# Softmax attention: the product of probabilities and values issued in two halves of 256 query columns

## The chip, the cores and the metric

The kernel runs on one core of one Trainium2 chip. The metric is the device time of one execution in microseconds (us), median of several runs. The profile is of one execution.

## The reference

Two blocks, each an attention-like mixer gated by a mixture of experts. The change touches only the softmax attention of the first block, on 8 sequences of 512 tokens, 128 features, 16 heads of 8:

```python
xn = _layernorm(x, axis=-1)
qkv = xn @ w_qkv + b_qkv                                   # 8 x 512 x 384
attn = jnp.einsum('bhqd,bhkd->bhqk', q, k) * hd ** (-0.5)  # hd = 8, 16 heads
attn = jax.nn.softmax(attn, axis=-1)
out = jnp.einsum('bhqk,bhkd->bhqd', attn, v)
s = out @ w_proj + b_proj
x = x + s * silu(experts(xn))
```

The second block is a linear attention with running sums and another set of experts.

## The kernel before, in words

The attention stage runs over 32 quarters u; a quarter is one sequence b and one group g of four heads. A loop `steps` calls `attend(u, g, b, now)` on each engine for u from -3 to 32; each engine has its own program, and semaphores order them. A quarter has four steps t (128 keys each), and a step has four pairs of scores, one for each head j; i = 4t + j counts pairs in a quarter.

In a pair TensorE issues two matmuls, on two different strips of 32 rows of its array: L1022 gives the scores of quarter u with keys on the partitions, 128 keys x 512 queries, in one of three banks (2, 3, 4); L1028 gives scores of quarter u + 2 with queries on the partitions, in one of three other banks (0, 1, 7). ScalarE turns the first into probabilities (L1297, `exp_set`). VectorE reduces the second to the negative row maxima (L1667, `max_set`), which go into the scores two quarters later as extra rows. The pair i may start when the exponential and the reduction of the pair three before it are done (`read_before`), since there are three banks of each.

The probabilities of a step are four tiles of 128 keys x 512 queries, in one of two buffers (t % 2). `output(u, g, t, even)` (L1119 to L1124) multiplies them with the values: four matmuls, one for each head, on four strips of 32 columns of the array, into the one bank 5, where they are added up over the four steps. The data are fp32, so that each matmul shows as two records. It is issued in step t + 1, behind the third pair (j == 2), and for t = 3 in the first step of the next quarter. It waits for the last exponential of its step, and the first of a quarter waits also until ScalarE has copied the accumulator of the quarter before (L1309, `o_read`). `pv_mm` counts the products; ScalarE waits for it before it overwrites a buffer of probabilities, and before the copy.

Behind the fourth pair of a step TensorE does other work of the stage: in t = 0 the transpose of the maxima (L1052); in t = 1 the transposes of the accumulator (L1066), which VectorE normalizes (L1691, L1693); in t = 2 and 3, depending on g, the projections of a later sequence (L324 to L326 through `project`), the projection of the values and its transposes (L1106), or transposes and the matmuls of the output projection (L1081, L1099). In the first and last quarters, filler matmuls (`keep_busy`, L1112) stand there too. VectorE also computes the low part of the maxima (m_lo, L1682) in t = 1, the low parts of projections (L1656) and the biased result (L1698). The order in each engine is fixed by hand as the code stands. GpSimd spreads tokens over experts' slots and splits the experts' weights meanwhile; SyncE's queue brings in the keys and queries of coming quarters.

Of the kernel before, what the change touches and what calls it, by code (L numbers as in the profile page):

```python
# [33 lines left out]
SEQ = 512  # L34
# [4 lines left out]
GROUPS = 4  # L39
# [7 lines left out]
def build(nc, x, w_qkv, b_qkv, w_proj, b_proj, router_w, w1, v1, w2, ffn_bias,  # L47
# [21 lines left out]
    with ctx:  # L69
# [3 lines left out]
        def sem(name):  # L73
            return ctx.enter_context(nc.semaphore(name))

        ps = ctx.enter_context(nc.psum_tensor("ps", [P, 8, 512], F32))
# [98 lines left out]
        def stage():  # L175
# [22 lines left out]
        probs = take(2, 4, SEQ)  # L198
# [9 lines left out]
        vaug = take(2, QT, HEADS, 32)  # L208
# [86 lines left out]
        st_mm, exp_set, pv_mm, o_read, oT_mm, onorm_set = (  # L295
            sem("st_mm"), sem("exp_set"), sem("pv_mm"), sem("o_read"), sem("oT_mm"), sem("onorm_set"))
# [88 lines left out]
        def bank_of(i):  # L385


            return 1 if i == 15 else i % 3

        def head_rows(tile, g, j):  # L390

            return tile[32 * j:32 * j + 32, g, :]

        def max_head(j):

            return (j + 2) % 4

        def read_before(i):

            return {0: -3, 1: 0, 2: -1, 15: 14}.get(i, i - 2)  # L400
# [510 lines left out]
        def _(pe):  # L911
# [90 lines left out]
            def attend(u, g, b, now):  # L1002
                v, g2 = u + 2, (g + 2) % GROUPS
                for t in range(4):
# [9 lines left out]
                    for j in range(4):  # L1014
                        i = t * 4 + j
                        if now.main:

                            if now.first and i == 0:
                                pe.wait_ge(e_set[0], 2)
                            if not (now.first and i < 3):  # L1020
                                pe.wait_ge(exp_set, u * 16 + read_before(i))
                            pe.matmul(ps[:, 2 + bank_of(i), :], head_rows(Ks, g, j)[:, t * P:(t + 1) * P],  # L1022
                                      head_rows(Qs, g, j), start=True, stop=True).then_inc(st_mm, 1)
                        if now.max:
                            if not (isinstance(v, int) and v * 16 + i < 3):
                                pe.wait_ge(max_set, v * 16 + read_before(i))
                            j2 = max_head(j)
                            pe.matmul(ps[:, (0, 1, 7)[bank_of(i)], :], head_rows(Qs, g2, j2)[:, t * P:(t + 1) * P],  # L1028
                                      head_rows(Ks, g2, j2), start=True, stop=True).then_inc(s_mm, 1)
                        if j == 2 and t == 0 and now.tail:  # L1030
                            output(u - 1, (g + 3) % GROUPS, 3, now.tail_even)
                        if j == 2 and t >= 1 and now.main:
                            if t == 1:

                                if not now.first:
                                    pe.wait_ge(o_read, u)
                                pe.wait_ge(vaug_set, b + 1)
                            output(u, g, t - 1, now.even)
                    if t == 0 and now.low:


# [15 lines left out]
                    if t == 1 and now.tail:  # L1057
# [7 lines left out]
                        for q in range(QT):  # L1065
                            mm = pe.transpose(ps[:, 6, q * P:(q + 1) * P], o_sb[:, q * P:(q + 1) * P], ident[:, :])  # L1066
# [5 lines left out]
                    if t == 2:  # L1072
# [5 lines left out]
                        if g == 0 and now.tail:  # L1078
                            pe.wait_ge(onorm_set, u)
                            for q in range(QT):  # L1080
                                mm = pe.transpose(ps[:, 6, q * P:(q + 1) * P], onorm[:, q, :], ident[:, :])  # L1081
# [10 lines left out]
                    if t == 3:  # L1092
# [3 lines left out]
                        if g == 0 and now.tail:  # L1096
                            pe.wait_ge(onT_set, b)
                            for q in range(QT):
                                mm = pe.matmul(ps[:, 6, q * P:(q + 1) * P], onT[:, q * P:(q + 1) * P], wproj[:, :],  # L1099
                                               start=True, stop=True)  # L1100
                            mm.then_inc(out_mm, 1)
                        if g == 3 and now.load:

                            pe.wait_ge(vT_set, b + 2)
                            for q in range(QT):
                                mm = pe.transpose(ps[:, 6, q * P:(q + 1) * P], vT[:, q * P:(q + 1) * P], ident[:, :])  # L1106
# [9 lines left out]
                split3(pe, ps[:, bank, :], wq_hi[:, which, :], wq_lo[:, which, :],  # L1116
                       seq_of(xT_hi, b), seq_of(xT_lo, b)).then_inc(proj_mm, 1)

            def output(u, g, t, even):  # L1119

                pe.wait_ge(exp_set, u * 16 + (4 * t + 4))
                for j in range(4):
                    mm = pe.matmul(ps[32 * j:32 * j + 32, 5, :], vaug[:, even, t, 4 * g + j, :],  # L1123
                                   probs[:, t % 2, j, :], start=(t == 0), stop=(t == 3))  # L1124
                mm.then_inc(pv_mm, 1)

# [127 lines left out]
            pe.wait_ge(pool_con, 19)  # L1256
            norm(0)
            steps(pe, attend)
            experts(0)
            pe.wait_ge(y_read[0], TILES)  # L1260
# [694 lines left out]
```

## Time and profile before

| | |
|---|---|
| median of 3 runs | 1088.25 us (1087.11 to 1091.65) |
| span of the profiled execution, first to last instruction | 1101.2 us |
| attention with products | from 86.9 to 473.9 us of it |
| busy shares, whole span | TensorE 89%, VectorE 77%, ScalarE 56%, GpSimd 52% |

The profile of the one execution gives its span, and no other time for it; the runs of the median were without a profile. Times of rows are us from the start of the span. Busy time of TensorE is the union of matmuls, whose ends are modelled. A granted clock of 1.00 is 2.4 GHz, one of 0.50 is 1.2 GHz.

### The profile page before, as it was taken

To read this page: it belongs to the slowest core of one execution; us is meant where nothing else is said; L and a number is where in the kernel's file an instruction comes from. 1 tells how busy PE (TensorE), PEld (TensorE's weight loads), DVE (VectorE), ACT (ScalarE), POOL (GpSimd) and SP (SyncE) were. 2 spreads that over 40 slices of the span, in tenths; PEclk is the share of its full clock that TensorE was granted. 3 is DMA by queue.
4 is the path that set the end of the run, shared out by engine and by line. 5 is a ranking of instruction groups with operands and counts; after the bars stand their busy time and mean duration, and the time that the engine had idled before them with its cause. 6 is when DMAs were issued, how large, how long until landed. Compare 5 with 4: busy or idle time off the path is not lost. (4 is left out here: it accounts for less than half of the span.)

```text
span 1101.2 us, 18065 instructions
## 1 busy us (share of the span) xinstructions
PE 980.5 (89%) x5608; PEld 634.8 (58%) x5608; DVE 852.7 (77%) x1910; ACT 620.6 (56%) x1248; POOL 572.2 (52%) x631
## 2 busy tenths in 40 slices
PE   5789999999999999989999964999996999999960
PEld 4542344343434344368888853756655888888850
DVE  7556899999979999435555548699992899999975
ACT  6115788888868888843333326333333666777642
POOL 7220687443435442015555556378782576777770
PEclk9995999999979999999999985699997999999985
DMA  6736566353535532216666635034312677687719
GB/s 209 300 104 193 160 193 209 101 169 113 170 101 170 178 116 88 87 58 195 207 197 187 205 95 146 20 108 126 93 44 82 180 214 208 208 224 220 218 56 236
DMA packets 121521, 170.37 MB, mean 155 GB/s; under 512 B 18801, under 2 KB 80594, under 8 KB 118354
## 3 DMA queue, kind: packets, MB, share of 16 engines
q1 hardware_dynamic: 94290, 110.94, 35.1%
q0 software_dynamic: 18688, 54.08, 14.3%
q10 hardware_dynamic: 8448, 4.20, 1.5%
q8 instruction: 45, 0.74, 0.3%
q14 instruction: 50, 0.41, 0.1%
HBM read 106.71 MB, written 63.76 MB: 155 GB/s over the span
## 5 line engine op out<-in xcount | busy, mean ns | idle before, releaser
L1667 DVE TENSOR_REDUCE nmax<-ps 128x1 f32<-128x512 f32 x512 | 324.8, 683 | 50.2 <-PE ps L1028 45.6
L1297 ACT ACTIVATE stage<-ps 128x512 f32<-128x512 f32 x512 | 274.4, 594 | 75.6 <-PE ps L1022 69.6
L841 POOL DMA_INDIRECT token_y<-stage,ids_now x184 | 182.7, 993 | 130.0 <-DVE stage L1723 58.3
L1028 PE MATMUL ps<-stage,stage 32*128 32x512 f32 x512 | 189.1, 521 | 14.1 <-DVE nmax L1667 12.8
L1022 PE MATMUL ps<-stage,stage 32*128 32x512 f32 x512 | 172.3, 496 | 9.0 <-ACT stage L1297 7.5
L797 POOL DMA_INDIRECT slots_x<-xn,pos x128 | 154.5, 1207 | 40.7 <-issue 39.6
L1168 PEld LDWEIGHTS ps<-stage,stage 128*128 128x128 f32 (+1 forms) x1288 | 164.9, 191 | 13.5 <-issue 1.8
L1168 PE MATMUL ps<-stage,stage 128*128 128x128 f32 (+1 forms) x1288 | 170.9, 275 | 1.5 <-issue 1.2
L1022 PEld LDWEIGHTS ps<-stage,stage 32*128 32x128 f32 x512 | 70.3, 188 | 158.0 <-ACT stage L1297 125.9
L324 PE MATMUL ps<-stage,stage 128*128 128x512 f32 x322 | 141.1, 438 | 3.6 <-issue 3.6
L1123 PE MATMUL ps<-stage,stage 128*32 128x512 f32 x1024 | 144.2, 637 | 0.0
L326 PE MATMUL ps<-stage,stage 128*128 128x512 f32 x322 | 127.8, 397 | 0.0
L325 PE MATMUL ps<-stage,stage 128*128 128x512 f32 x322 | 127.1, 395 | 0.0
L1350 ACT ACTIVATE stage<-ps 128x512 f32<-128x512 f32 (+1 forms) x69 | 41.2, 597 | 104.8 <-PE ps L326 83.0
L1028 PEld LDWEIGHTS ps<-stage,stage 32*128 32x128 f32 x512 | 75.6, 194 | 37.7 <-DVE nmax L1667 30.2
L1787 DVE TENSOR_TENSOR stage<-ps,stage 128x512 f32<-128x512 f32 (+1 forms) x69 | 47.5, 689 | 61.6 <-PE ps L326 36.9
L1352 ACT ACTIVATE stage<-ps,ebcol 128x512 f32<-128x512 f32 x92 | 63.2, 687 | 52.8 <-PE ps L326 24.1
L1791 DVE SCALAR_TENSOR_TENSOR stage<-stage,stage 128x512 f32<-128x512 f32 x92 | 71.3, 774 | 23.3 <-ACT stage L1355 16.9
L326 PEld LDWEIGHTS ps<-stage,stage 128*128 128x128 f32 x322 | 59.8, 186 | 15.6
L324 PEld LDWEIGHTS ps<-stage,stage 128*128 128x128 f32 x322 | 60.4, 188 | 11.9 <-issue 2.3
L325 PEld LDWEIGHTS ps<-stage,stage 128*128 128x128 f32 x322 | 60.4, 187 | 8.2
L1355 ACT ACTIVATE stage<-ps,ebcol 128x512 f32<-128x512 f32 x92 | 63.2, 687 | 0.6 <-PE ps L326 0.6
(226 smaller groups left out, 1537.4 us busy)
## 6 DMA issues: line engine op xcount, KB each, us to landing
stage<-halves_w SPq DMA_DIRECT2D x23, 1024.0 KB
stage<-halves_w SPq DMA_DIRECT2D x23, 704.0 KB
stage<-slots_x SPq DMA_DIRECT2D x46, 260.0 KB
stage<-q_halves SPq DMA_DIRECT2D x32, 256.0 KB
halves_w<-stage POOLq DMA_DIRECT2D x16, 512.0 KB
k_halves<-stage SPq DMA_DIRECT2D x24, 256.0 KB
q_halves<-stage SPq DMA_DIRECT2D x24, 256.0 KB
stage<-k_halves SPq DMA_DIRECT2D x128, 48.0 KB
```

The costliest lines, as they stand in the source:

```text
L324: pe.matmul(out_ap, w_hi_ap, x_hi_ap, start=start, stop=False)
L325: pe.matmul(out_ap, w_hi_ap, x_lo_ap, start=False, stop=False)
L326: return pe.matmul(out_ap, w_lo_ap, x_hi_ap, start=False, stop=stop)
L797: pool.indirect_dma_start(out=slots_x[L], out_offset=bass.IndirectOffsetOnAxis(ap=pos[:, c:c + 1], axis=0), in_=xn[:, t, :], in_offset=Non ...
L841: pool.indirect_dma_start(out=token_y, out_offset=bass.IndirectOffsetOnAxis(ap=ids_now[:, r, q:q + 1], axis=0), in_=ysb[:, r, q, :], in_of ...
L1022: pe.matmul(ps[:, 2 + bank_of(i), :], head_rows(Ks, g, j)[:, t * P:(t + 1) * P], head_rows(Qs, g, j), start=True, stop=True).then_inc(st_m ...
L1028: pe.matmul(ps[:, (0, 1, 7)[bank_of(i)], :], head_rows(Qs, g2, j2)[:, t * P:(t + 1) * P], head_rows(Ks, g2, j2), start=True, stop=True).th ...
L1123: mm = pe.matmul(ps[32 * j:32 * j + 32, 5, :], vaug[:, even, t, 4 * g + j, :], probs[:, t % 2, j, :], start=(t == 0), stop=(t == 3))
L1168: mm = pe.matmul(ps[:, 5 + r, q * P:(q + 1) * P], hT[0:M, par, q * P:(q + 1) * P], wdn[0:M, r, f, :], start=(f == 0 and q == 0), stop=(f = ...
L1297: act.activation(probs[:, t % 2, j, :], ps[:, 2 + bank_of(i), :], ACT.Exp, scale=SCALE).then_inc(exp_set, 1)
L1667: dve.tensor_reduce(nmax[:, g % 2, at:at + 1], ps[:, (0, 1, 7)[bank_of(i)], :], AX, ALU.max, negate=True).then_inc(max_set, 1)
L1791: dve.scalar_tensor_tensor(hT[:, par, :], gsig[:, par, :], 1.0, gact[:, par, :], ALU.add, ALU.mult).then_inc(h_set[L], 1)
```

## The change

Each product is issued in two halves: query columns 0 to 255 behind the second pair (j == 1), columns 256 to 511 behind the fourth (j == 3), in the same step as before. A half has four matmuls of 256 columns. The wait for the exponentials stands before the first half, `pv_mm` is increased after the second. Only the first half of the first step starts the accumulation; only the second half of the last ends it. The work that stood behind the fourth pair now stands behind the second half.

```diff
-                        if j == 2 and t == 0 and now.tail:
-                            output(u - 1, (g + 3) % GROUPS, 3, now.tail_even)
-                        if j == 2 and t >= 1 and now.main:
-                            if t == 1:
+                        if j in (1, 3) and t == 0 and now.tail:
+                            output(u - 1, (g + 3) % GROUPS, 3, now.tail_even, j // 2)
+                        if j in (1, 3) and t >= 1 and now.main:
+                            if t == 1 and j == 1:
 
                                 if not now.first:
                                     pe.wait_ge(o_read, u)
                                 pe.wait_ge(vaug_set, b + 1)
-                            output(u, g, t - 1, now.even)
+                            output(u, g, t - 1, now.even, j // 2)
...
-            def output(u, g, t, even):
-
-                pe.wait_ge(exp_set, u * 16 + (4 * t + 4))
+            def output(u, g, t, even, part):
+
+                if part == 0:
+                    pe.wait_ge(exp_set, u * 16 + (4 * t + 4))
+                c = slice(part * SEQ // 2, (part + 1) * SEQ // 2)
                 for j in range(4):
-                    mm = pe.matmul(ps[32 * j:32 * j + 32, 5, :], vaug[:, even, t, 4 * g + j, :],
-                                   probs[:, t % 2, j, :], start=(t == 0), stop=(t == 3))
-                mm.then_inc(pv_mm, 1)
+                    mm = pe.matmul(ps[32 * j:32 * j + 32, 5, c], vaug[:, even, t, 4 * g + j, :],
+                                   probs[:, t % 2, j, c], start=(t == 0 and part == 0), stop=(t == 3 and part == 1),
+                                   skip_group_check=True)
+                if part == 1:
+                    mm.then_inc(pv_mm, 1)
```

## Rows read from the trace of the kernel before

**Rows 1.** The page: the span, and the granted clock in 40 slices (tenths).

```profile
span 1101.2 us, 18065 instructions
...
PEclk9995999999979999999999985699997999999985
```

**Rows 2.** Windows of the attention stage: stretch, length, busy us, granted clock.

```profile
88.00:108.00 20.00, 18.80 (x81) 5.90 (x77) 11.69 (x21) 9.59 (x19) 2.07 (x4) 0.50 0.60 185
116.00:304.00 188.00, 183.36 (x1192) 76.01 (x1190) 174.63 (x313) 154.68 (x305) 109.27 (x136) 1.00 0.52 159
...
320.00:442.00 122.00, 118.48 (x780) 49.41 (x776) 113.81 (x204) 101.04 (x199) 46.79 (x53) 1.00 0.43 132
```

Behind the length stand TensorE, its weight loads, VectorE, ScalarE and GpSimd, then the clock, DMA share and GB/s.

**Rows 3.** Groups of lines, 148 to 292 us: busy, mean ns, idle before.

```profile
L1667 DVE TENSOR_REDUCE nmax<-ps 128x1 f32<-128x512 f32 x195 | 123.5, 683 | 8.3 <-PE ps L1028 5.9 <-issue 1.5
L1297 ACT ACTIVATE stage<-ps 128x512 f32<-128x512 f32 x195 | 104.6, 593 | 20.0 <-PE ps L1022 17.2 <-issue 0.6
```

**Rows 4.** Timeline of TensorE, a plain step: start, length, line, idle before.

```profile
254.47 0.50 PE L1028 MATMUL ps<-stage,stage 32*128 32x512 f32 x1
254.90 1.07 PE L1123 MATMUL ps<-stage,stage 128*32 128x512 f32 x8
255.90 0.49 PE L1022 MATMUL ps<-stage,stage 32*128 32x512 f32 x1
...
257.64 1.07 PE L1123 MATMUL ps<-stage,stage 128*32 128x512 f32 x8
...
259.07 0.28 PE L1052 MATMUL ps<-ident,nmax 128*16 128x128 f32 x1
259.28 0.50 PE L1022 MATMUL ps<-stage,stage 32*128 32x512 f32 x1
```

**Rows 5.** Timeline of VectorE over the same steps.

```profile
251.46 0.25 DVE L1691 RECIPROCAL rden<-ps 128x16 f32<-128x16 f32 x1
...
251.94 4.27 DVE L1667 TENSOR_REDUCE nmax<-ps 128x1 f32<-128x512 f32 x7
256.46 2.57 DVE L1667 TENSOR_REDUCE nmax<-ps 128x1 f32<-128x512 f32 x4 [0.25 <-PE ps L1028]
```

**Rows 6.** Timeline of TensorE: transposes of the maxima, one a quarter (four of them).

```profile
116.19 0.28 PE L1052 MATMUL ps<-ident,nmax 128*16 128x128 f32 x1
...
295.25 0.28 PE L1052 MATMUL ps<-ident,nmax 128*16 128x128 f32 x1
...
324.53 0.28 PE L1052 MATMUL ps<-ident,nmax 128*16 128x128 f32 x1
...
441.83 0.27 PE L1052 MATMUL ps<-ident,nmax 128*16 128x128 f32 x1
```

**Rows 7.** Timeline of TensorE, a step at the half clock.

```profile
91.06 1.94 PE L1123 MATMUL ps<-stage,stage 128*32 128x512 f32 x8
92.92 0.79 PE L1022 MATMUL ps<-stage,stage 32*128 32x512 f32 x1
...
94.53 0.79 PE L1028 MATMUL ps<-stage,stage 32*128 32x512 f32 x1
95.25 1.94 PE L1123 MATMUL ps<-stage,stage 128*32 128x512 f32 x8
```

**Rows 8.** Timeline of TensorE: a projection behind the fourth pair.

```profile
169.37 0.51 PE L324 MATMUL ps<-xT_hi,wq_hi 128*128 128x512 f32 x1
...
170.27 0.50 PE L1022 MATMUL ps<-stage,stage 32*128 32x512 f32 x1
...
170.61 0.39 PE L1022 MATMUL ps<-stage,stage 32*128 32x512 f32 x1
```

**Rows 9.** Timeline of TensorE's weight loads: those of one product.

```profile
252.02 0.16 PEld L1123 LDWEIGHTS ps<-stage,stage 128*32 128x32 f32 x8 [0.24 <-issue]
```

**Rows 10.** Timeline of TensorE: filler matmuls in the last quarters.

```profile
458.45 0.73 PE L1112 MATMUL ps<-xT_hi,wq_hi 128*128 128x512 f32 x2
459.12 0.69 PE L1022 MATMUL ps<-stage,stage 32*128 32x512 f32 x3
```

## The prediction

> **What bounds the kernel now.** I read the page first [rows 1]: one span of 1101.2 us, and TensorE's granted clock at 9 or more of 10 in nearly all slices, with a slice of 5 at the start of the attention stage (slice 4, 82 to 110 us) and one of 7 in its middle (slice 12). Then the windows of the attention stage [rows 2]. At the full clock, 116 to 304 us and 320 to 442 us, TensorE shows 97% busy, VectorE 93%, ScalarE 82%. Three engines so close together say that none is alone the bound: the work goes in a loop through them. The groups of lines [rows 3] say where VectorE stops: its reduction (L1667) takes 683 ns, and what ends most of the idle time before it is a score matmul of TensorE (L1028). ScalarE's exponential (593 ns) waits for TensorE longer still. So I read the timeline of TensorE through one plain step, a step being the four pairs of scores of one t [rows 4].
>
> The loop is this. The last pair before the product (L1123) starts at 254.47; the product starts 0.43 us later, at 254.90, when that pair is done. The next pair starts 1.00 us after it, at 255.90, and takes 0.49. VectorE has run seven reductions in one train without a gap (251.94, 4.27 us) and then has nothing for 0.25 us: its next one begins at 256.46 [rows 5], 0.07 after the pair's end. Its reduction takes 0.68, and the third pair after may only start then, because there are three banks for each kind of score. 0.43 + 1.00 + 0.49 + 0.07 + 0.68 = 2.67 us, and the products stand 2.74 apart (254.90, 257.64); what is left, 0.07, is the release's (I use 0.05 below). The seven reductions give a pitch of (4.27 - 0.68) / 6 = 0.60 us, so four take 2.40. A plain step is thus 0.3 us longer than VectorE needs, and the whole product standing between two pairs is the reason: three banks cover 1.8 us, and from the release of the pair before the product to the data of the pair behind it 0.43 + 1.00 + 0.49 + 0.12 = 2.04 us pass.
>
> **What a half costs.** No row shows a product of 256 columns. But the whole one stands at both levels of the clock: 1.00 us from its start to the next pair at 2.4 GHz [rows 4] and 92.92 - 91.06 = 1.86 us at 1.2 GHz [rows 7]. The part that goes with the clock is the difference, 0.86 us at the full clock, and 0.14 stays. A half is then 0.43 + 0.14 = 0.57 us, at the half clock 0.86 + 0.14 = 1.00. Bounds: 0.50 (everything halves) and 1.00 (nothing does). I take 0.57, since 86% of the whole was seen to follow the clock, as streamed columns do.
>
> The change adds 128 blocks (32 quarters, four products each). Each further block needs the pair before it drained: 0.43 from that pair's start [rows 4], where pairs otherwise follow at once or at 0.2 to 0.3. What this comes to if it is not hidden is a part of rival (a).
>
> **The plain step after the change.** First half behind the second pair: that pair starts when the reduction three before is done (call it 0, plus 0.05); half from 0.48 to 1.05; third pair's data at 1.54, wanted by VectorE at 1.80. Fourth pair: released at 1.20, so it starts at 1.25; second half 1.68 to 2.25; next pair's data at 2.74, wanted at 3.00. Both come 0.26 us early, so VectorE sets the pace: 2.40 to 2.45 for 2.74, a gain of 0.30. The first half has to wait for the fourth exponential of the step before, which the third pair waited for anyhow; with ScalarE's pitch (under 0.6) it ends near 0.3, before 0.48. Behind this wait stand the third pair's matmuls of both kinds and all that follows; they are hidden by the same 0.26.
>
> Written as a chain from the fourth pair: 0.43 + 0.57 + X + 0.49 + 0.07 + 0.60 + 0.05 = 2.21 + X, where X is what TensorE does behind the step's last pair. The maxima's transpose gives X = 0.21 (259.07 to 259.28 [rows 4]): 2.42, still a gain of 0.30. The projection gives 170.27 - 169.37 = 0.90 [rows 8], so 3.11. Before, TensorE's own path there is 0.43 + 1.00 + 0.43 + 0.90 + 0.33 = 3.09 (0.33 is the step from the first two pairs to a third, 170.27 to 170.61 [rows 8]). These steps win nothing; the same holds for the others with X of 0.6 to 1.1 (transposes, out projection).
>
> Steps of four quarters: 16. Four have t = 1, where VectorE adds m_lo, the reciprocal and the normalization (251.46 to 251.94 is 0.48 us for the latter two [rows 5]) and is the bound already: nothing. Six at t = 2 or 3 have a large X (two projections, the value projection and its transposes, two steps of the output path): nothing. Six are plain or have X = 0.21: 6 x 0.30 = 1.8 us per four quarters. At the full clock with the reductions running lie 15 quarters from 116.19 to 295.25 and 10 from 324.53 to 441.83 [rows 6]: 25 / 4 x 1.8 = 11.3 us.
>
> **At the half clock** [rows 7] products stand 4.19 apart (91.06, 95.25). After: a pair's drain is 0.72 (94.53 to 95.25), so 2 x 0.72 + 2 x 1.00 = 3.44, with some 0.15 for a trailing pair 3.6: a gain of 0.6 a step. The stretch at the start holds at least 20 us at 0.50 [rows 2], 20 / 4.19 = 4.8, five steps. In the middle, the two quarters from 295.25 to 324.53 [rows 6] are 5.4 us longer than two at the mean of the fifteen before ((295.25 - 116.19) / 15 = 11.94); at 4.19 - 2.74 = 1.45 a step that is 3.7, of which I count three: 3.0 + 1.8 us.
>
> **The rest at nothing.** In the last two quarters there are no reductions, and TensorE puts filler matmuls behind the last pairs, X = 459.12 - 458.45 = 0.67 [rows 10]; by the chain 2.21 + 0.67 = 2.88, by TensorE's path of now 2.19 + 0.67 = 2.86, so nothing either way. Instruction issue: 16 more matmuls and weight loads a step; a product's eight loads lie within 0.16 us now [rows 9], so more of them lie under the streaming; were they not hidden, it would be 2 x 0.16 us a step, which only case (a) counts. ScalarE's wait for the product before it overwrites the probabilities: the second half ends 0.6 after the fourth pair, while the fourth exponential ends then too. The copy of the accumulator (L1309) may come 0.1 later, once in a quarter, with 0.2 to spare. The queues of SyncE and GpSimd are not passed by anything; they are paced by the quarters and were not late. No DMA is added.
>
> **Sum.** 11.3 + 3.0 + 1.8 = 16 us less than the profiled 1101.2 us. That execution is 13 us longer than the median of 1088.25 without a profile; the difference lies around the kernel as a whole, so I take the same 16 us off the median: 1072.
>
> **Rivals.** (a) A half is not cheap: if fixed cost or drain makes it 1.00 us, the chain is 2.64 + X, so a plain step gains 0.1 and each of six steps with large X loses 0.43, t = 1 another 0.1: 2.6 + 0.4 - 0.6 = 2.4 us per four quarters, 15 us, and at the half clock 2 x 0.72 + 2 x 1.86 = 5.2 against 4.2, 8 us: 1111. At its strongest, with TensorE the bound throughout, each further block adds its drain and fixed part whole: 128 x (0.43 + 0.14) = 73 us, 1161; of that I make 1%, because VectorE's unbroken trains [rows 5] show TensorE waiting for it. The Trainium skill bears on this in TensorEngine Tiling, Key Properties: a change of tiling mode drains the engine. It gives no figure for it; by it alone the 1161 would be the answer, and the trace agrees with the rule as such, with the 0.43 us in front of a product [rows 4]. It decides from a half of 0.72 us, where 6 x 0.15 gained and 6 x 0.15 lost cancel. For it: TensorE is shown 97% busy. Against: the two clock levels. 12%. (b) The gain is real but given back: the waits are not where the hand-made schedule has them (the first half waits 0.15 for an exponential or the accumulator's copy, the steps with large X lose as much as the plain ones win). It leaves 1083 to 1093, no change. 18%. (c) VectorE becomes the full bound: its idle time of 188 - 174.6 = 13.4 and 122 - 113.8 = 8.2 us [rows 2] goes entirely, and with 5 at the half clock 27 us: 1061. For it: the pace is slack by 0.26 in plain steps; against: the projections stand behind the fourth pair as before. 10%. (d) The clock. It fell to 1.2 GHz in slice 12 [rows 1] and rose again, which cost the 5.4 us worked out above. The new order may lose such a stretch or get another; this moves any of the cases by 5.4, and 4% is for a larger effect of it. The forecast itself, 1064 to 1080, gets 56%.
>
> **How the numbers follow.** 0.5% is 5.4 us, about what a measurement of this kernel can tell from no change. Faster by more: the forecast, (c) and part of (b) and (d), 0.70; within: most of (b), 0.17; slower: (a) and parts of (b) and (d), 0.13. The range 1059 to 1087 leaves out (a) and half of (b); the forecast alone is 1064 to 1080.
>
> **What the profile after would show.** Right: L1123 in blocks of 256 columns, about 0.57 us from start to the next pair, two a step; the quarters by the start of L1052 about 0.45 us shorter on average at the full clock, the plain quarter most (some 0.9); VectorE's idle time before L1667 cut by more than half; projection steps unchanged. Wrong: halves of 0.7 us or more; TensorE waiting for ScalarE in front of the first half; the reductions' trains broken at the same places; half-clock stretches elsewhere than now.

## The result, and the profile after

The change made the kernel slower: 1109.97 us median (1108.55 to 1112.81, 4 runs) against 1089.71 (1087.11 to 1091.65, 4 runs), a ratio of 1.0193 with a 95% interval of 1.0162 to 1.0224. I had forecast 1072, with 1059 to 1087 as the range. The page of the changed kernel, its span and clock slices:

```profile
span 1111.1 us, 20111 instructions
...
PEclk9559999999999999999999985689998999999985
```

The span is only 9.9 us above that of [rows 1], half of what the medians say. The slice of 5 at 82 to 110 us and the slice of 7 are not there in this execution, while slices 2 and 3, ahead of the attention stage, are at 5. The profiled execution of before ran the start of the attention stage at the half clock: its fifth transpose of the maxima starts at 128.50 us, that of the changed kernel at 118.60, and of the eleven traces below only that of e8 has such a start. So the stage has to be compared where both stand at the full clock. The timeline of TensorE in the changed kernel, the transposes of the maxima (L1052), one a quarter, through four quarters:

```profile
246.47 0.28 PE L1052 MATMUL ps<-ident,nmax 128*16 128x128 f32 x1
...
257.36 0.28 PE L1052 MATMUL ps<-ident,nmax 128*16 128x128 f32 x1
...
270.81 0.28 PE L1052 MATMUL ps<-ident,nmax 128*16 128x128 f32 x1
...
283.91 0.28 PE L1052 MATMUL ps<-ident,nmax 128*16 128x128 f32 x1
...
296.52 0.28 PE L1052 MATMUL ps<-ident,nmax 128*16 128x128 f32 x1
```

The plain quarter takes 257.36 - 246.47 = 10.89 us where it took 11.37, and that is the gain that was forecast, in part. The other three take 13.45, 13.10 and 12.61, where they took 12.33, 12.20 and 11.65. The pattern repeats: the next four run from 296.52 to 346.39, 49.87 us, against 295.25 - 247.70 = 47.55 before. That is 2.3 us lost in every four quarters; at this rate it is some 16 us over the 27 from the fifth transpose to the last (an estimate: both traces have dips of the clock in that stretch). The windows of these two stretches (columns as in [rows 2]), the kernel before first, then the changed one:

```profile
247.70:295.25 47.55, 46.20 (x304) 19.11 (x302) 44.23 (x80) 39.22 (x78) 21.08 (x24) 1.00 0.48 152
```

```profile
296.52:346.39 49.87, 47.87 (x434) 20.87 (x430) 44.13 (x80) 38.80 (x78) 21.01 (x24) 1.00 0.46 145
```

The clock is full in both, VectorE does the same work (44.2 and 44.1 us), and what grew is its idle time: from 3.3 to 5.7 us. The two last quarters, to the output projection's matmuls, take 484.31 - 457.99 = 26.3 us against 477.64 - 453.31 = 24.3: 2 us more. What is left of the 20 us I have not placed. (One experiment below, e2, has no interval, because most of its runs were disturbed, slower ones.)

The change of length of single things came as forecast. This is the timeline of TensorE over the third and fourth steps of a quarter with projections (L1125 is the product, L324 to L326 the projection):

```profile
262.55 0.64 PE L1125 MATMUL ps<-stage,stage 128*32 128x256 f32 x8
263.12 0.50 PE L324 MATMUL ps<-xT_hi,wq_hi 128*128 128x512 f32 x1
...
264.02 0.49 PE L1022 MATMUL ps<-stage,stage 32*128 32x512 f32 x1
...
264.46 0.64 PE L1125 MATMUL ps<-stage,stage 128*32 128x256 f32 x8
265.03 0.50 PE L1022 MATMUL ps<-stage,stage 32*128 32x512 f32 x1
...
265.84 0.49 PE L1022 MATMUL ps<-stage,stage 32*128 32x512 f32 x1 [0.31 <-ACT stage L1301]
266.58 0.50 PE L1028 MATMUL ps<-stage,stage 32*128 32x512 f32 x1 [0.25 <-DVE nmax L1671]
267.01 0.64 PE L1125 MATMUL ps<-stage,stage 128*32 128x256 f32 x8
267.58 0.51 PE L324 MATMUL ps<-xT_hi,wq_hi 128*128 128x512 f32 x1
...
268.48 0.49 PE L1028 MATMUL ps<-stage,stage 32*128 32x512 f32 x1
```

A half takes 265.03 - 264.46 = 0.57 us from its start to the next pair, which is the forecast's price to the hundredth. But look at 266.58: the last pair of the quarter, pair 15, waits for a reduction (L1671), and only behind it come the second half (267.01), then the projection (267.58), then the pair that VectorE is waiting for (268.48). VectorE's timeline over the same steps:

```profile
264.58 0.69 DVE L1671 TENSOR_REDUCE nmax<-ps 128x1 f32<-128x512 f32 x1 [0.71 <-PE ps L1028]
265.19 0.74 DVE L1660 SCALAR_TENSOR_TENSOR stage<-ps,cols,stage 128x512 fp32r<-128x512 f32 x1
265.85 1.96 DVE L1671 TENSOR_REDUCE nmax<-ps 128x1 f32<-128x512 f32 x3
269.05 0.69 DVE L1671 TENSOR_REDUCE nmax<-ps 128x1 f32<-128x512 f32 x1 [1.24 <-PE ps L1028]
```

And the same two places of the kernel before, which [rows 8] leads up to, TensorE first:

```profile
171.16 1.06 PE L1123 MATMUL ps<-stage,stage 128*32 128x512 f32 x8
172.15 0.50 PE L1022 MATMUL ps<-stage,stage 32*128 32x512 f32 x1
172.84 0.50 PE L1028 MATMUL ps<-stage,stage 32*128 32x512 f32 x1 [0.19 <-issue]
173.27 0.51 PE L324 MATMUL ps<-xT_hi,wq_hi 128*128 128x512 f32 x1
```

```profile
218.44 0.69 DVE L1667 TENSOR_REDUCE nmax<-ps 128x1 f32<-128x512 f32 x1 [0.48 <-PE ps L1028]
...
222.32 0.69 DVE L1667 TENSOR_REDUCE nmax<-ps 128x1 f32<-128x512 f32 x1 [0.66 <-PE ps L1028]
```

Before, the whole product (171.16) ran ahead of pair 15 and filled its wait. VectorE's gaps at the two places grew from 0.48 to 0.71 and from 0.66 to 1.24 us, and the second grew by one half of a product. In the next quarter the gaps went from 0.48 and 0.35 to 0.71 and 0.92 (once 1.23, in the quarter of 13.10 us above), in the one after from 0.18 and 0.40 to 0.41 and 0.96. In sum the gaps that the timeline shows grew by 2.5 us in four quarters. At the plain quarter there is now one gap, of 0.34, at its end. Before there were two, the 0.25 of [rows 5] and one of 0.17 in the first step behind it; the changed kernel first, then the kernel before:

```profile
255.62 3.21 DVE L1671 TENSOR_REDUCE nmax<-ps 128x1 f32<-128x512 f32 x5 [0.34 <-issue]
```

```profile
259.20 1.34 DVE L1667 TENSOR_REDUCE nmax<-ps 128x1 f32<-128x512 f32 x2 [0.17 <-PE ps L1028]
```

**Theory A** from this: the second half stands in series between a late release and the data that VectorE waits for. **Theory D**, its sharper form: what makes it dear is the irregular order of banks. The three banks go round as i % 3 within a quarter of 16 pairs, so pair 15 takes bank 1, which pair 13 had (`read_before(15) = 14`), and pair 1 of the next quarter takes it again (`read_before(1) = 0`). These two pairs may start only when the reduction two pairs back is done; VectorE then has 1.20 us of work left, not 1.80. My prediction had three back for all. **Rival B**: the 128 further drains and fills. **Rival C**: the added instructions.

### The profile page after: what moved, and what is told of

Its sections match the earlier page's. It is cut to its first block and busy times, and to the rows that moved or that the text cites. A ratio compares the mean times of both kernels' runs of the same rounds, so it can differ in the third digit from the quotient of the medians.

```text
span 1111.1 us, 20111 instructions
## 1 busy us (share of the span) xinstructions
PE 982.2 (88%) x6630; PEld 647.4 (58%) x6632; DVE 852.9 (77%) x1910; ACT 615.3 (55%) x1248; POOL 568.3 (51%) x631
## 5 line engine op out<-in xcount | busy, mean ns | idle before, releaser
L1671 DVE TENSOR_REDUCE nmax<-ps 128x1 f32<-128x512 f32 x512 | 323.6, 682 | 53.0 <-PE ps L1028 46.4
L1028 PE MATMUL ps<-stage,stage 32*128 32x512 f32 x512 | 185.1, 515 | 14.6 <-DVE nmax L1671 13.8
L1125 PE MATMUL ps<-stage,stage 128*32 128x256 f32 x2048 | 164.4, 393 | 7.0 <-ACT stage L1313 6.2
L1022 PE MATMUL ps<-stage,stage 32*128 32x512 f32 x512 | 159.3, 497 | 7.3 <-ACT stage L1301 6.6
L324 PE MATMUL ps<-stage,stage 128*128 128x512 f32 x322 | 141.0, 438 | 3.6 <-issue 3.6
L326 PE MATMUL ps<-stage,stage 128*128 128x512 f32 x322 | 127.6, 396 | 0.0
L1022 PEld LDWEIGHTS ps<-stage,stage 32*128 32x128 f32 x512 | 64.6, 182 | 104.5 <-issue 52.7
L1028 PEld LDWEIGHTS ps<-stage,stage 32*128 32x128 f32 x512 | 74.5, 188 | 33.1 <-DVE nmax L1671 26.0
L1356 ACT ACTIVATE stage<-ps,ebcol 128x512 f32<-128x512 f32 x92 | 62.9, 684 | 48.7 <-PE ps L326 20.4
L1125 PEld LDWEIGHTS ps<-stage,stage 128*32 128x32 f32 x2048 | 40.5, 108 | 71.5 <-issue 57.2
L1795 DVE SCALAR_TENSOR_TENSOR stage<-stage,stage 128x512 f32<-128x512 f32 x92 | 64.0, 695 | 20.4 <-ACT stage L1359 14.2
L326 PEld LDWEIGHTS ps<-stage,stage 128*128 128x128 f32 x322 | 59.6, 185 | 15.7
L324 PEld LDWEIGHTS ps<-stage,stage 128*128 128x128 f32 x322 | 60.4, 188 | 11.9 <-issue 2.3
```

Source lines behind the costliest of these rows:

```text
L324: pe.matmul(out_ap, w_hi_ap, x_hi_ap, start=start, stop=False)
L326: return pe.matmul(out_ap, w_lo_ap, x_hi_ap, start=False, stop=stop)
L1125: mm = pe.matmul(ps[32 * j:32 * j + 32, 5, c], vaug[:, even, t, 4 * g + j, :], probs[:, t % 2, j, c], start=(t == 0 and part == 0), stop=( ...
L1671: dve.tensor_reduce(nmax[:, g % 2, at:at + 1], ps[:, (0, 1, 7)[bank_of(i)], :], AX, ALU.max, negate=True).then_inc(max_set, 1)
L1795: dve.scalar_tensor_tensor(hT[:, par, :], gsig[:, par, :], 1.0, gact[:, par, :], ALU.add, ALU.mult).then_inc(h_set[L], 1)
```

## The experiments

Four quarters stand for the sum of four successive intervals of the maxima's transpose (L1052), read from each run's timeline of TensorE, with a granted clock of 1.00 in the windows of all but e2. At the full clock most kernels repeat it within 0.2 us; the changed kernel shows 49.7 to 50.3, e4 46.9 to 48.5. The ratios are to runs of the kernel before taken with each kernel (medians 1088.86 for e1 to e4, 1088.79 for e5 to e8, 1087.23 for e9 to e11).

| kernel | median us | ratio to before (95%) | four quarters us |
|---|---|---|---|
| before | 1089.71 | | 47.55 |
| changed | 1109.97 | 1.0193 (1.0162 to 1.0224) | 49.87 |
| e1, halves behind 2nd and 3rd pair | 1131.27 | 1.0348 (1.0306 to 1.039) | 51.44 |
| e2, whole behind the 4th | 1179.91 | none | 61.43, clock below 1.00 |
| e3, both halves behind the 3rd | 1091.9 | 1.003 (1.0012 to 1.0047) | 47.63 |
| e4, changed, rotating banks | 1085.99 | 0.9968 (0.9953 to 0.9983) | 47.25 |
| e5, before, rotating banks | 1078.24 | 0.9893 (0.9835 to 0.995) | 46.48 |
| e6, whole in 4th steps | 1095.43 | 1.0054 (1.002 to 1.0088) | 48.25 |
| e7, halves where free | 1090.8 | 1.0001 (0.9972 to 1.0031) | 47.52 |
| e8, e7 with rotating banks | 1075.96 | 0.9849 (0.9805 to 0.9894) | 45.78 |
| e9, e1 with rotating banks | 1114.72 | 1.0201 (1.0116 to 1.0286) | 50.06 |
| e10, whole in 1st steps | 1108.55 | 1.0179 (1.0104 to 1.0254) | 49.45 |
| e11, two steps, rotating banks | 1077.48 | 0.988 (0.9824 to 0.9936) | 46.13 |

**e1: the second half ahead of the fourth pair.**

```diff
-                        if j in (1, 3) and t == 0 and now.tail:
+                        if j in (1, 2) and t == 0 and now.tail:
...
-                        if j in (1, 3) and t >= 1 and now.main:
+                        if j in (1, 2) and t >= 1 and now.main:
...
-                            output(u, g, t - 1, now.even, j // 2)
+                            output(u, g, t - 1, now.even, j - 1)
```

> The second half goes behind the third pair instead of the fourth; the first stays behind the second, and there are as many blocks and drains as in the changed kernel. Theory A (series): the changed kernel loses because its second half (0.57 us) stands behind the fourth pair, in series with the pair's late release and with the other work there. Then the gaps of VectorE in the fourth steps go back from 1.24, 0.92 and 0.96 us to about those of before (0.66, 0.35, 0.40) or less, and the time is 1075 to 1090 us, no slower than before. Rival B (drains): it loses because of the 128 further drains and fills of 0.57 us. Then it stays at 1105 to 1112.

Measured 1131.27 us: slower still, outside the ranges of both. VectorE's timeline in the steps with projections:

```profile
271.77 0.69 DVE L1671 TENSOR_REDUCE nmax<-ps 128x1 f32<-128x512 f32 x1 [0.63 <-PE ps L1028]
...
275.64 0.69 DVE L1671 TENSOR_REDUCE nmax<-ps 128x1 f32<-128x512 f32 x1 [0.65 <-issue]
```

Theory A's own part came in: the gap of the fourth step is 0.65, as before, not 1.24. But new gaps of about 0.3 us opened elsewhere, five of them in four quarters, and TensorE's timeline shows what stands there:

```profile
268.31 0.64 PE L1125 MATMUL ps<-stage,stage 128*32 128x256 f32 x8
268.88 0.50 PE L1022 MATMUL ps<-stage,stage 32*128 32x512 f32 x1
...
269.31 0.64 PE L1125 MATMUL ps<-stage,stage 128*32 128x256 f32 x8
269.88 0.50 PE L1022 MATMUL ps<-stage,stage 32*128 32x512 f32 x1
...
270.31 0.50 PE L324 MATMUL ps<-xT_hi,wq_hi 128*128 128x512 f32 x1
```

The third and the fourth pair now stand alone, each drained for 0.43 us ahead of other work. The number of blocks is that of the changed kernel; the number of separately drained groups of scores in a step is three, not two (**theory F**). Counting blocks alone, as rival B and my own prediction did, misses this.

**e2: the whole product behind the fourth pair.**

```diff
-                        if j == 2 and t == 0 and now.tail:
+                        if j == 3 and t == 0 and now.tail:
...
-                        if j == 2 and t >= 1 and now.main:
+                        if j == 3 and t >= 1 and now.main:
```

> The kernel before with its whole product moved from behind the third pair to behind the fourth; no further block or drain. Theory A: a whole product of 1.00 us now stands in series behind the fourth pair, so the gaps of VectorE grow in every step: by about 1.0 us in the fourth steps, 0.65 in the third, and plain steps come to 2.64 + X against 2.74: some 4 to 5 us per four quarters, 30 to 40 us in all, 1115 to 1130. Rival B: 1088 to 1092, as before, since the number of blocks is that of before.

Measured 1179.91 us (1160.2 to 1190.72). Rival B, which had no change, is excluded as the whole story: with the blocks of before, merely standing behind the fourth pair, the product costs 70 us even in the shortest execution. Theory A had the sign and at most half the size (1115 to 1130). A part of what it missed is its own sum: the quarters whose clock stayed at 1.00 are 12.35 and 14.17 us long, where the kernel before has 11.37 and 11.65, 3.5 us more in two quarters where theory A had 4 to 5 in four. VectorE's gap in a third step with a projection is at its forecast (0.48 + 0.65):

```profile
292.84 0.69 DVE L1667 TENSOR_REDUCE nmax<-ps 128x1 f32<-128x512 f32 x1 [1.14 <-PE ps L1028]
```

Another part is the clock. The profiled execution is the one of 1190.72 us. In the quarter ahead of the two shown here the clock was 1.00, with TensorE busy for 9.97 of 12.35 us; then it falls:

```profile
285.09:301.76 16.67, 13.99 (x80) 4.95 (x76) 12.30 (x22) 10.30 (x20) 5.25 (x6) 0.85 0.33 95
301.76:320.00 18.24, 16.09 (x80) 5.88 (x77) 10.44 (x19) 10.30 (x20) 5.25 (x6) 0.67 0.53 164
```

**e3: the two halves back to back where the whole stood.**

```diff
-                        if j in (1, 3) and t >= 1 and now.main:
+                        if j == 2 and t >= 1 and now.main:
...
-                            output(u, g, t - 1, now.even, j // 2)
+                            output(u, g, t - 1, now.even, 0)
+                            output(u, g, t - 1, now.even, 1)
```

(and so for t == 0.)

> Both halves back to back behind the third pair, where the whole product stood: the added matmuls and weight loads without added drains. Both theories: 1088 to 1092, no change, since the two halves stream into each other (the last product of the changed kernel, where both stood together, took 1.07 us against 1.06 for the whole). If the added instructions themselves cost (rival C, issue), each product is 0.1 us or more longer and the time 1100 or more.

Measured 1.003, 3 us for some thousand more matmuls and as many weight loads; the four quarters are 47.63 us, 0.08 more, so most of the 3 us lies elsewhere. Rival C, which had 1100 or more, is out. The changed kernel's last product, where both halves stand together, shows the same in its timeline:

```profile
479.50 1.07 PE L1125 MATMUL ps<-stage,stage 128*32 128x256 f32 x16
```

**e4: the changed kernel with banks that rotate on through the quarters.**

```diff
         def bank_of(i):
 
 
-            return 1 if i == 15 else i % 3
+            return i % 3
...
         def read_before(i):
 
-            return {0: -3, 1: 0, 2: -1, 15: 14}.get(i, i - 2)
+            return i - 2
...
-                            pe.matmul(ps[:, 2 + bank_of(i), :], head_rows(Ks, g, j)[:, t * P:(t + 1) * P],
+                            pe.matmul(ps[:, 2 + bank_of(u * 16 + i), :], head_rows(Ks, g, j)[:, t * P:(t + 1) * P],
...
-                            pe.matmul(ps[:, (0, 1, 7)[bank_of(i)], :], head_rows(Qs, g2, j2)[:, t * P:(t + 1) * P],
+                            pe.matmul(ps[:, (0, 1, 7)[bank_of(v * 16 + i)], :], head_rows(Qs, g2, j2)[:, t * P:(t + 1) * P],
```

(and the same two on the readers' side.)

> The changed kernel, but the three banks of each kind of score rotate on through the quarters, so that the last pair of a quarter waits for the reduction three pairs back as all others do, not two back (the pair 15 took bank 1 after pair 13). Theory A in its narrow form (D: the series hurts because pair 15 is released late): the gaps of VectorE in the fourth steps (1.24, 0.92, 0.96) shrink by 0.4 to 0.6 each, to those of the third steps, about 7 to 12 us in all: 1098 to 1103. Theory A without it: a gap shrinks only where pair 15 was seen to wait, by under 0.2, and the time stays at 1105 to 1110.

Measured 1085.99, 24 us below the changed kernel, twice the narrow theory's most. Excerpts of VectorE's timeline:

```profile
252.51 0.69 DVE L1671 TENSOR_REDUCE nmax<-ps 128x1 f32<-128x512 f32 x1 [0.73 <-PE ps L1028]
253.12 0.74 DVE L1660 SCALAR_TENSOR_TENSOR stage<-ps,cols,stage 128x512 fp32r<-128x512 f32 x1
253.78 2.64 DVE L1671 TENSOR_REDUCE nmax<-ps 128x1 f32<-128x512 f32 x4
256.34 0.74 DVE L1660 SCALAR_TENSOR_TENSOR stage<-ps,cols,stage 128x512 fp32r<-128x512 f32 x1
...
285.93 6.06 DVE L1671 TENSOR_REDUCE nmax<-ps 128x1 f32<-128x512 f32 x10
```

The gap of 1.24 us is gone altogether (a train of four runs into the low part of the projection at 256.34), and the plain quarter has a train of ten. The gap of the third step stands, 0.73. So the late release is the dear part. My expectation was too small for a reason that these rows show: with three back, pair 15 is released ahead of the low part of the projection (253.12 to 253.78), so that VectorE has that 0.65 us of work behind the release as well as a third reduction, 2.45 us in all, and the whole 1.24 goes, not 0.6 of it. The 0.34 at the end of the plain quarter goes too.

**e5: the kernel before with the rotation alone.** The edit is that of e4 on the kernel before.

> The kernel before (whole product behind the third pair) with the banks rotating on through the quarters. Theory D (the late release of pair 15 costs because half a product and the other work now stand behind it): in the kernel before the whole product was issued ahead of pair 15 and filled its wait, so taking the wait away gives little, 0 to 5 us: 1084 to 1089. Rival E (the release of pair 15 is a cost of its own, in any order, and the rotation would have given the kernel before the same 24 us as the changed one): 1063 to 1068.

Measured 1078.24: 10.6 us gained, between the ranges of D and E. The late release cost the kernel before something as well, 47.55 - 46.48 = 1.1 us in four quarters, but less than half of the 2.6 us that it cost the changed one. With the whole product ahead of pair 15 the rest was hidden. The same two runs say how much of the loss hangs on the order of the banks. With the old order the change costs 20.3 us (2.32 in four quarters), with the rotating one 1085.99 - 1078.24 = 7.8 us (0.77). So about two thirds of the loss come with the irregular order of banks, and a third does not.

**e6: the changed kernel with the whole product in the fourth steps.**

```diff
+            def halved(t, g):
+
+                return t != 3
...
-                        if j in (1, 3) and t >= 1 and now.main:
+                        if (j in (1, 3) if halved(t, g) else j == 2) and t >= 1 and now.main:
...
-                            output(u, g, t - 1, now.even, j // 2)
+                            output(u, g, t - 1, now.even, j // 2 if halved(t, g) else None)
```

(part None is the whole product.)

> The changed kernel, but in the fourth steps (t = 3) the product goes out whole behind the third pair, as before; in the other three steps in halves. Banks as before. Theory D: the 0.57 us that each fourth step lost goes away and its plain ones keep 0.1: per four quarters 49.9 - 1.8 = 48.1 us, 12 us in all, 1095 to 1100; the rest of the loss stays in the third steps, where 0.23 us a step was lost to the serial half. Rival B (the added drains, the same in each step): a quarter of them goes, so a quarter of 21 us: 1103 to 1107.

Measured 1095.43 and 48.25 us: theory D's numbers, not rival B's. Four of sixteen steps held 70% of the loss.

**e7: halves only where nothing, or only the transpose of the maxima, stands behind the fourth pair.** `halved` returns `t == 0 or (t >= 2 and g == 1)`.

> Halves only in steps with nothing or only the maxima's transpose behind the fourth pair: all with t = 0, and t = 2 and 3 of the quarters with g = 1 (6 of 16 steps); whole behind the third pair elsewhere. Banks as before. Theory A: these steps win 0.1 to 0.3 us each and none loses: per four quarters about 1 us, 7 us in all, 1079 to 1086. Rival B: six sixteenths of the loss of 21 us stay: 1094 to 1098.

Measured 1.0001 (0.9972 to 1.0031): no change, where theory A had 1079 to 1086 and rival B 1094 to 1098. The plain quarter is shorter by 0.47 us, 10.90, and the others together lose as much, 12.59, 12.12 and 11.91. These halves do not gain with the banks as they are. VectorE's timeline at the end of the plain quarter, where pair 15's late release stands ahead of a half:

```profile
198.55 3.21 DVE L1675 TENSOR_REDUCE nmax<-ps 128x1 f32<-128x512 f32 x5 [0.34 <-PE ps L1028]
```

**e8: e7 with rotating banks.**

> The run before this one, with the rotating banks as well. Theory D: both gains add, the fourth step of g = 1 too is free of the late release: 1072 to 1082. If the whole products need the bank order of before, or the halves gain only where the rotation lets them, it is no faster than the changed kernel with rotation alone (1086).

Measured 1075.96, ratio 0.9849 (0.9805 to 0.9894), inside theory D's range, and the kernel is faster than both given ones. But "both gains add" is not what happened, since e7 had none: these halves gain only with the rotation, 46.48 - 45.78 = 0.7 us in four quarters against e5, and the medians of the two are not told apart. VectorE now runs through the plain quarter and the first step behind it in one train:

```profile
245.92 7.97 DVE L1675 TENSOR_REDUCE nmax<-ps 128x1 f32<-128x512 f32 x13
```

**e9: e1 with rotating banks.**

> Halves behind the second and the third pair (the first run) with rotating banks. Theory F: that order was slow because it leaves three drained groups of scores in a step (the first two pairs, the third alone, the fourth alone) in place of two, so that TensorE needs 3 x 0.43 + 2 x 0.57 = 2.43 us plus the other work behind the fourth pair, and a half stands behind every pair but the first and fourth. Rotation frees only pairs 15 and 1, so four quarters go from 51.4 to 48.5 to 50.5 us and it stays slower than the changed order with rotation (47.25 us, 1086): 1098 to 1122. If instead the late releases (theory D) were its whole loss too, it would come to 1086 or below.

Measured 1114.72 and 50.06 us, inside theory F's ranges. The rotation took 1.4 us from four quarters, and 2.8 us more remain than in e4, which has the same blocks and the same banks but two drained groups in a step. Gaps of 0.31 stand as in e1, this one in front of a reduction of a second step:

```profile
248.13 0.69 DVE L1671 TENSOR_REDUCE nmax<-ps 128x1 f32<-128x512 f32 x1 [0.31 <-PE ps L1028]
```

So the order with a third group has a cost of its own that the banks do not explain.

**e10: the changed kernel with the whole product in the first steps.** `halved` returns `t != 0`.

> The changed kernel, but in the first steps of the quarters (t = 0) the product goes out whole behind the third pair. Banks as before. Theory D: pair 1 is released two reductions back as pair 15 is (both sides of the same irregular bank), and the first half behind it costs 0.05 + 0.43 + 0.57 + 0.49 + 0.07 - 1.20 = 0.4 us at most, against 0.2 with the whole behind the third pair: 0.1 to 0.25 us a quarter, 3 to 7 us in all: 1103 to 1107. If the first step gains by halves, as the prediction had it (0.30 a quarter), this run is 9 us slower than the changed kernel: 1119.

Measured 49.45 us for four quarters, 0.42 below the changed kernel: theory D's sign at its small end, 0.1 us a quarter for the half behind pair 1. The 1108.55 us in all is above its range by 1.5 us and not told apart from the changed kernel, but far from the 1119 that the prediction's price would give.

**e11: rotating banks and halves in only two of sixteen steps.** `halved` returns `t >= 2 and g == 1`.

> The kernel before with rotating banks (1078) and halves only in t = 2 and 3 of the quarters with g = 1: 2 of 16 steps. Theory D with the prediction's price: 0.30 us for each such step when no pair is released late, so four quarters go from 46.48 to 45.9 us, 4 us in all: 1073 to 1076. Beside the run with halves in all first steps too (45.78 us, 1076) it shows what halves in t = 0 bring with rotation: the prediction's 0.30 a step would make this run 1.2 us a four quarters slower than that one, 8 us: 1084.

Measured 1077.48 and 46.13 us. Two halved steps bring 0.35 in four quarters, 0.17 each; the four first steps of e8 bring another 0.35, 0.09 each. The prediction's 0.30 a step is too much in both places, also with no pair released late. VectorE's timeline says why. The one gap that e11 has and e8 does not is in the first step behind the plain quarter:

```profile
244.26 1.33 DVE L1675 TENSOR_REDUCE nmax<-ps 128x1 f32<-128x512 f32 x2 [0.24 <-PE ps L1028]
```

The other three first steps have no such gap in e5 or in e11, so as far as the timelines show, e8's 0.35 is the gain of one step and not of four.

## Why the prediction was wrong, point by point

**The bound now.** Right: the loop through the three engines, 2.72 us for 2.74 seen, and the product standing between two pairs.

**What a half costs.** Right: 0.57 us forecast, 0.57 measured. Reading the fixed part off the two clock levels worked. So the rival (a) that I gave 12% was right in its sign and wrong in its cause; the kernel is slower with cheap halves, and that (a)'s 1111 is 1 us from the measured time is luck. The 0.72 us from which I let (a) decide does not follow from its own chain either: a plain step of 1.64 + 0.72 = 2.36 us would still gain 0.3; by that chain gains and losses cancel near 0.75.

**The plain step.** The step that failed first: "that pair starts when the reduction three before is done", used for all pairs. It holds for pairs 3 to 14. Pairs 15 and 1 wait for two before (and pairs 0 and 2 for four), which `bank_of` and `read_before` say in two lines of the code, and the changed order puts a half directly behind each of them. Pair 15's is the dear one; the half behind pair 1 costs about 0.1 us a quarter (e10). With the right count, VectorE's gap behind a fourth pair is 0.05 + 0.43 + 0.57 + X + 0.49 + 0.07 - c, with c, the work that VectorE has left at the release, 1.80 for three back and 1.20 for two. For the third step with a projection (X = 0.90) this is 0.71, measured 0.71; for the fourth 1.31, measured 1.24; with the transposes (X = 0.59) in the third 0.40, measured 0.41, in the fourth 1.00, measured 0.92. With 1.00 in place of 0.57 it gives 1.14 for e2's third step, measured 1.14. That the order of banks makes most of the loss was shown by the rotation: with it in both kernels the change costs 7.8 us, without it 20.3.

**Steps with a large X, "these steps win nothing".** The second failed step; its part in the third steps does not need the banks. I compared two sums of TensorE's path (3.11 and 3.09). But before, the chain of such a step is released at the third pair, and in the third steps VectorE had the reciprocal and the normalization still to do behind that release; after, it is released at the fourth pair, with those behind it. The gap grew by 0.23 in each of the third steps, and e4, without late releases, keeps the gap of 0.73. In VectorE's timelines with rotating banks, the third steps have 0.7 us more of gaps in e4 than in e5, the fourth steps 0.6 more, the plain quarter 0.5 less. Together this is the 0.77 us that the change still costs there. With the late release on top, six steps with a large X in four quarters lost 0.23 to 0.58 us each.

**The gain of 0.30 in six steps.** Mis-sized. The gap of [rows 5] is that of one plain step, and I gave its worth to six. In four quarters VectorE's timeline of before shows only two gaps in these six steps, 0.25 and the 0.17 at 259.20: of my 1.8 us about 0.4 was there to be won. In the third step of the plain quarter VectorE still has the normalization to do, and in three of the four first steps it does not wait. Where it does wait the arithmetic held: with rotating banks the halves close both gaps (e8's train of 13), which were 0.25 and 0.24 us in e5; by the starts of L1052 they are worth 0.35 each.

**The half clock, 4.8 us.** Wrong basis. The stretch at 1.2 GHz at the start of the stage belonged to the one profiled execution; the changed kernel's has none there, and in the middle of the stage it has two quarters with a mean clock of 0.89 and 0.88. I also put the 13 us between the span and the median to "the kernel as a whole"; the start of the stage alone differs by 9.9 us between the two traces.

**The rest at nothing.** The added instructions: 3 us (e3), not nothing, small. The copy of the accumulator "with 0.2 to spare": TensorE does wait for it in front of the first half of t = 1, at 258.56 for 0.43 us in the changed kernel. VectorE's timeline has no gap from 255.62 to 263.87, so in that quarter the wait was hidden; no run takes it away by itself. The last two quarters lost 2 us.

**Rival (b)**, the gain given back, had the right place in half a sentence ("the steps with large X lose as much as the plain ones win") and was priced at no change; they lose about 2.8 us in four quarters where the plain quarter wins 0.5. The Trainium skill's rule in TensorEngine Tiling, Key Properties, that a change of mode drains the engine, did not decide this change: the trace agrees with the rule (0.43 us ahead of a half as ahead of a whole), but the added blocks stood where pairs of scores could drain together. e1 and e9 show a case where it counts.

What stays open: the 2 us or so outside the quarters, where most of e3's 3 us lies, and how much of e2 is the clock.

## What to carry to other kernels

Before moving work between two places of a ring of buffers, write down for each place how far back its release lies, from the code, not from the rule that most of the places follow; an irregular place (here one in sixteen, and its partner) can hold most of the cost. Before counting a gain at several places, look at the bounding engine's gap at each of them, since a gap read in one step is not there in all that look alike. Work placed ahead of a late-released instruction is hidden by its wait; work placed behind it is added to the next consumer's gap. And count not only the blocks of another tiling that a step has but the groups of work between them, since each group is drained once.

## What the runs showed of the hardware that I had not expected

A product of eight 32-column matmul records of 256 columns costs 0.57 us from start to the next scores, one of 512 costs 1.00, and two halves issued together cost what the whole does (1.07 against 1.06 us shown). A pair of scores standing alone ahead of a product costs the same 0.43 to 0.44 us as two pairs that start together: in e1, 268.88 to 269.31 for one, in the changed kernel 264.02 to 264.46 for two.
